# ScalarE scales the keys of a linear-attention block, one activation per head, in place of VectorE's broadcast product

## The reference, cut to what matters

```python
qkv = einsum('bnd,ed->bne', x, w_qkv)      # x: layer-normed rows, 6250 x 256; 8 heads of 64
q, k, v = split(qkv), each to heads        # b h n d
k = instance_norm(k)                       # over the 64 of a head, each row by itself
v = instance_norm(v)
dots = einsum('bhnd,bhne->bhde', k, v)     # 64 x 64 for each head, summed over all rows
out = einsum('bhnd,bhde->bhne', q, dots) / N
return einsum('bne,de->bnd', out, w_out) + b_out
```

## Time and profile before

| | |
|---|---|
| median of 3 runs | 3259.44 us (3259.29 to 3263.07) |
| the profiled execution | 3257.38 us |
| its span in the trace | 3255.6 us |
| instructions | 54447 |

### The profile page before, as it was taken

One profiled execution on the slowest core, in us unless ns is written; L12 is line 12 of the kernel. 1 busy time (PEld: TensorE's weight loads), 2 busy tenths in 40 slices (PEclk: granted clock), 3 DMA queues, 4 the chain that ended last, 5 costly groups with the idle time before them and its releaser, 6 DMA issues. The chain is left out here.

```text
span 3255.6 us, 54447 instructions
## 1 busy us (share of the span) xinstructions
PE 2608.8 (80%) x16782; PEld 1852.5 (57%) x16782; DVE 2002.2 (61%) x4822; ACT 1307.5 (40%) x2213; POOL 169.9 (5%) x160
## 2 busy tenths in 40 slices
PE   0666556485758888887759999999799999976997
PEld 0334333342335445443338888888688888864665
DVE  8878899989989899899932222222122222236555
ACT  0333222234656666677761222222122212235666
POOL 0000000000000000000000000000011111114000
PEclk9888778687889999999969999999899999988999
DMA  5000000013313323233334444444544444410000
GB/s 162 0 0 1 0 1 0 10 38 117 132 58 126 109 108 128 98 117 125 122 103 141 148 150 144 150 141 154 184 135 137 133 139 132 140 51 30 26 26 28
DMA packets 153846, 304.75 MB, mean 94 GB/s; under 512 B 28963, under 2 KB 125476, under 8 KB 153700
## 3 DMA queue, kind: packets, MB, share of 16 engines
q1 hardware_dynamic: 101796, 217.44, 21.2%
q10 hardware_dynamic: 51776, 85.24, 7.2%
q0 software_dynamic: 128, 0.26, 0.0%
HBM read 196.54 MB, written 106.37 MB: 93 GB/s over the span
## 5 line engine op out<-in xcount | busy, mean ns | idle before, releaser
L1079 PE MATMUL banks<-outer,ring 128*128 128x257 f16 x2450 | 544.4, 274 | 15.4 <-DMA outer<-table,heavy 8.4
L1079 PE MATMUL banks<-tabs,ring 128*128 128x257 f16 x2450 | 541.6, 273 | 8.4 <-DMA ring<-counts 8.4
L1080 PE MATMUL banks<-outer,ring 128*128 128x256 f16 x2450 | 544.2, 273 | 0.0
L1080 PE MATMUL banks<-tabs,ring 128*128 128x256 f16 x2450 | 541.5, 272 | 0.0
L744 ACT ACTIVATE ring<-banks 128x512 f16<-128x512 f32 x637 | 382.4, 600 | 378.5 <-POOLq L605 376.8
L1048 PE MATMUL banks<-ring 128*128 128x512 f16 x1102 | 343.4, 425 | 138.2 <-SPq L504 66.1
L745 ACT ACTIVATE banks<-banks 128x512 f32<-128x512 f32 x637 | 384.1, 603 | 0.0
L1655 DVE TENSOR_SCALAR ring<-val,outer 128x512 f16<-128x512 f16 x1102 | 316.3, 346 | 21.0 <-PE banks L1048 20.9
L1048 PEld LDWEIGHTS banks<-ring 128*128 128x128 f16 x1102 | 153.2, 147 | 300.3 <-issue 260.5
L1079 PEld LDWEIGHTS banks<-outer,ring 128*128 128x128 f16 x2450 | 238.8, 97 | 48.9 <-DMA outer<-table,heavy 8.7
L1079 PEld LDWEIGHTS banks<-tabs,ring 128*128 128x128 f16 x2450 | 238.2, 97 | 41.5 <-issue 9.2
(11 more groups left out here) (340 smaller groups left out, 3483.0 us busy)
## 6 DMA issues: line engine op xcount, KB each, us to landing
ring<-counts SPq DMA_DIRECT2D x98, 800.0 KB, 4.7
counts<-ring ACTq DMA_DIRECT2D x84, 896.0 KB, 4.0
ring<-counts SPq DMA_DIRECT2D x98, 768.0 KB, 4.1
tabs<-in_fw SPq DMA_DIRECT2D x4, 2048.0 KB, 9.7
outer<-in_x SPq DMA_DIRECT2D x5, 1280.0 KB, 13.5
outer<-in_x SPq DMA_DIRECT2D x25, 256.0 KB, 2.8
residual<-outer SPq DMA_DIRECT2D x25, 256.0 KB, 2.2
table<-tabs SPq DMA_DIRECT2D x25, 256.0 KB, 2.6
```

Of the source, the lines that this page charges most:

```text
L1079: mm(o[:, 0:D + 1], a, xtab[l][:, cb, D:2 * D + 1], start=cb == 0, stop=False)
L1080: m = mm(o[:, 0:D], a, xtab[l][:, cb, 0:D], start=False, stop=cb == NT - 1)
```

## The change

VectorE's block ends with the reciprocal, which now raises a new semaphore, `k_scales`. ScalarE waits for it and multiplies the k half of each tile of the window in place, head by head: eight activations of 128x64 with the function Copy and the factor, a column of `mix_small`, as scale. In the row windows 0 to 10 they stand right behind the root of the same window. That of window 11 and those of the rounds stand behind the first half's eviction of the next round, ahead of that round's window. The last one stands between the root and the copy of the keys.

```diff
+        s_kinv = sem("k_scales")
...
+            def k_scaled(w):
+
+                if WINDOWS[w]:
+                    n = windows_before(w)
+                    act.wait_ge(s_kinv, n + 1)
+                    act.wait_ge(s_kvc, WSTART[w + 1])
+                    for t in range(WSTART[w], WSTART[w + 1]):
+                        k = n % 2 * 120 + 96 + (t - WSTART[w]) * 8
+                        for h in range(HEADS):
+                            kh = kv[t % 4][:, h * DH:(h + 1) * DH]
+                            ins = act.activation(kh, kh, ACT.Copy, scale=msc[:, k + h:k + h + 1])
+                        ins.then_inc(s_kn, 1)
...
             for w in range(ROW_WINDOWS):
                 window(w)
                 kv_stds(w)
+                if w < ROW_WINDOWS - 1:
+                    k_scaled(w)
...
                 ins.then_inc(s_evict, 1)
                 w = ROW_WINDOWS + n
+                k_scaled(w - 1)
                 window(w)
...
             kv_stds(ROW_WINDOWS + ROUNDS - 1)
+            k_scaled(ROW_WINDOWS + ROUNDS - 1)
             act.activation(hkeys, sort[home[ROUNDS]], ACT.Copy).then_inc(s_conv, 1)
...
                 dve.wait_ge(s_kvs, n + 1)
-                link(dve.reciprocal(msc[:, b + 96:b + 96 + c], msc[:, b + 72:b + 72 + c]))
-                for t in range(WSTART[w], WSTART[w + 1]):
-                    k = b + 96 + (t - WSTART[w]) * 8
-                    dve.wait_ge(s_kvc, t + 1)
-                    kg = kv[t % 4][:, 0:512].rearrange("p (g e) -> p g e", e=DH)
-                    dve.tensor_tensor(kg, kg, msc[:, k:k + 8].unsqueeze(2).to_broadcast([P, 8, DH]), op=ALU.mult).then_inc(s_kn, 1)
+                dve.reciprocal(msc[:, b + 96:b + 96 + c], msc[:, b + 72:b + 72 + c]).then_inc(s_kinv, 1)
```

## The result

The changed kernel takes 3272.97 us (median of 7 runs, 3269.93 to 3276.36), the kernel before 3259.98 us in the same comparison (7 runs). The ratio is 1.004, 95% interval 1.003 to 1.005: slower by 13.0 us, more than a measurement of this kernel needs to tell it from no change. The forecast was 3273.5 us. The total was right to half a microsecond, its terms were not: the row windows lost more than forecast, and the rounds and what follows them gave more back. The profiled execution's span is 3271.2 us against 3255.6.

What follows compares the result with a forecast made beforehand. Row windows were taken to be bound by a ring of waits, the rounds mostly by VectorE. Row windows +18.6 and rounds -4.5 gave +14.1 on 3257.38, 3271.5; the median's 2.06 more made 3273.5 us, range 3264 to 3290.

Steps and rivals of the forecast that it cites:

- What bounds a row window: Row windows 0 to 11: a ring of waits sets their length, 17.50 us, not VectorE, busy 13.70 us of it.
- the ring: Row windows: reciprocal, scaled keys, dots, next kv products queued behind them, squares, second reduction, next root and reciprocal; 17.50 us.
- Spacing of the activations, 0.25 us: ScalarE's 128x64 activations: one starts 0.25 us after another, derived from 128x1024 activations with one pointer.
- the lower bound, 0.17: Lowest spacing of ScalarE's activations, 0.17 us, from the 16-column root without a pointer, with 48 columns more.
- The row windows, +18.6: Eleven row windows that hand on to a next one, each 1.69 us longer: +18.6 us.
- My 5.90 us from the reciprocal to the kv products: Row windows after the change: from the reciprocal's end to the end of the dots, where kv products start, 5.90 us.
- the 4.21 of before: Row windows before the change: the kv products start 4.21 us after the reciprocal's end, read from one window's timeline.
- my rival on the clock: Row windows: TensorE's longer idle time drops its clock; all eleven at 0.77 add 10 us, 3284 us; chance 0.12.
- The rounds, -4.4 up to the last reciprocal: Column rounds: later dots cost time in rounds 0 and 2, VectorE's removed products save more in later rounds; -4.4 us.
- R + 8.47: Even rounds with three tiles: TensorE has done the dots 8.47 us after the reciprocal's end R.
- Behind the last window, -0.1: After the last window: the copy of the keys on ScalarE stands behind 16 activations and eats VectorE's 1.2 us; -0.1 us.
- The sum: Sort stage: row windows +18.6 and rounds with what follows -4.5, together +14.1 us.

Runs made afterwards that it cites:

- e1: The changed kernel, but VectorE multiplies the keys in row windows 0 to 10 as before; ScalarE scales them in window 11 and the rounds: 3245.57 us.
- e3: The kernel before, with each window's dots behind the next window's kv products in TensorE's queue, row windows only: 3223.66 us.
- e9: The changed kernel with dots behind the next kv products and scaling moved into ScalarE's wait for the second kv product, both in row windows: 3190.23 us.
- e10: The changed kernel with VectorE's product in row windows 0 to 10 and, in row windows, dots behind the next window's kv products: 3208.76 us.
- e7: The kernel before, with five products of zeros ahead of each window's dots in row windows 1 to 11: 3240.63 us.
- e8: The changed kernel, with seven products of zeros ahead of each window's dots in row windows: 3246.54 us.
- e11: As e9, with the dots in rounds 0, 2, 4, 6 and 8 waiting for the next, long round: 3190.87 us.
- e2: The changed kernel, but ScalarE scales only in row windows 0 to 10; VectorE multiplies in window 11 and the rounds: 3285.51 us.
- e5: The changed kernel with one activation of 128x512 per tile instead of eight of 128x64, all heads getting head 0's factor: 3238.75 us.

## Why the prediction was right, point by point

- **What bounds a row window.** Right. Giving the row windows back to VectorE brings back 198.2 us (e1), cutting the ring saves 39 (e3), and the same activations off the ring no longer lengthen a window: there they beat VectorE's product by 14 us (e9 against e10).
- **Spacing of the activations, 0.25 us.** 0.239 measured: 16 in 3.93 us instead of 4.10. Taken from the pair with one pointer operand, it was off by 5%; the lower bound, 0.17 from an instruction without a pointer, was no candidate.
- **The row windows, +18.6.** +23.9 measured, by two errors of opposite sign, -1.3 and +6.6. My 5.90 us from the reciprocal to the kv products held: 5.69 in the first window, 5.89 in the other ten. But the 4.21 of before, read from one window, was 4.29 in the mean, so this part is 17.3 us. And I had held the clock as it was, and it did not stay: the first kv products took on average 4.64 us (3.60 to 4.89) where those of before took 4.04 (3.60 to 4.92), 0.6 x 11 = 6.6 us. This is most of my rival on the clock, to which I gave 0.12 as a case of its own with +10. It was not a case beside the forecast; it came together with it. I had also written there that these rows show the clock low in some windows only. They show more: the dots of each window run at the low level for all or most of their time, 3.2 to 3.6 us from their start to the kv products for what takes 1.9 in e7. That hid a part of the scaling's price, since the slow dots of tile 0 lie beside the scaling of tile 1. With the clock held the same step costs 2.35 us a window (e8 against e7), not 1.6, so the clock as a whole did not add to the difference between the kernels.
- **The rounds, -4.4 up to the last reciprocal.** -9.3. Round by round, forecast and measured: round 0 +1.5 and +2.2, round 2 +0.4 and -1.2, round 4 -1.8 and -2.5, round 6 0 and -0.5, round 8 -1.8 and -3.0, round 10 -0.3 and -0.9, rounds 12 and 13 together -2.4 and -3.4. The dots done at R + 8.47 held well enough: the turning starts 8.15 us after R in round 3 and 8.45 in round 5. What I had put at nothing is the length of the turning behind them. TensorE's dots now end right where the turning begins, and the turning runs at a higher clock: 1.91 us in round 3 instead of 3.15, 1.91 in round 7 and 1.97 in round 9 instead of 3.68 each. In e11, where the dots are elsewhere, round 3 is back at 3.68 and round 9 at 3.57. Round 1 goes the other way, 2.75 instead of 1.97, which is what round 0 lost beyond my 1.5. And the turning of round 5 follows TensorE's own dots without idle time, where I had written that it would wait for VectorE.
- **Behind the last window, -0.1.** -4.3. The wait for the copy of the keys is there, 1.16 us instead of the 1.0 that my arithmetic held. But the piece products behind the dots (the matmuls of L934 to L939 in the kernel before) now follow with no idle time, take 7.2 us instead of 10.6 and are done when VectorE comes for them; before, VectorE waited 3.66 us. The rows, first of the kernel before, then of the changed one, with the stretch of the piece products (granted clock 0.50 and 0.99):

```profile
658.18 0.29 DVE L1436 COPY outer<-banks 128x128 f32<-128x128 f32 x1 [3.66 <-PE banks L939]
...
647.58:658.14 10.56, 10.56 (x69) 5.53 (x70) 6.93 (x30) 0.00 (x0) 0.00 (x0) 0.50 0.01 2
```

```profile
662.33 4.26 DVE L1444 TENSOR_SCALAR outer<-val,outer 128x128 f16<-128x128 f16 x17 [1.16 <-ACT tabs L753]
...
671.38 0.29 DVE L1449 COPY outer<-banks 128x128 f32<-128x128 f32 x1
...
664.18:671.35 7.17, 7.17 (x69) 4.25 (x68) 7.15 (x23) 0.00 (x0) 1.84 (x1) 0.99 0.01 2
```

- **The sum.** By the terms the sort stage should have ended 14.1 us later. It was +23.9 - 9.3 - 4.3 = +10.3, and 1.6 by the first kv product's clock. The last 3.8 us between the spans lie in stages that the change doesn't touch, which differ by as much between other runs. The half microsecond between forecast and result is luck, and so is that the size came out at 14: the row windows were 5.3 us above their term, the rounds 4.9 and the part behind them 4.2 below theirs. The sign is not luck: e1 and e2 show a loss in the row windows that is larger than the gain in the rounds.

Open is what makes the row windows settle at 20.48 us rather than somewhere else: the kv product lengthens by ever smaller steps with the same idle time before it. The runs show that filling the idle time ends it (e8), not how the chip decides.

## What to carry to other kernels

Before work is moved to an idler engine, find the ring: who waits in whose queue for the moved step. Here VectorE's busy time fell by 33 us and the time rose by 13, because the step stood between a reciprocal and products queued behind its consumer; with the consumer queued later and the step put into a wait of its new engine, the same activations were part of a kernel 70 us faster (e9), of which the later dots alone gave 37 (e3). Price a run of small instructions by their spacing, not by their columns: 400 of 64 columns took 96 us of ScalarE, and 50 of 512 would have taken 31 (as in e5, where one factor serves all eight heads, so the scaling by head is left out).

## What the runs showed of the hardware that I had not expected

TensorE's dropped clock costs nearly as much as a badly placed step. Products of zeros in its waits, doing nothing for the result, took 19 us off the kernel before (e7) and 26 off the changed one (e8); in the row windows, where they stand, it is 22.5 and 20.8. With them the granted clock of a row window was 1.00 instead of 0.77 to 0.90, and the same 16 dots took 1.9 us instead of 3.4. And a step that delays TensorE can pay by it: where the dots ended right ahead of the next burst, that burst was faster, in rounds 3, 7 and 9 with 1.9 us instead of 3.2 to 3.7 for 16 transposes, and 7.2 us instead of 10.6 for the piece products. It did not always pay in full: in round 5 the transposes took 2.81 us instead of 3.29, and in round 1 they took longer, 2.75 instead of 1.97.
